# A graph kernel on one core: the node passes in sequence, x rows stored during the counting, messages weighed by column, and a small memset with a wait behind some gathers

## The chip, the cores and the metric

One NeuronCore of one Trainium2 chip. The metric is the device time of the whole kernel in microseconds (us), the median of several executions. The engines are PE (TensorE), DVE (VectorE), ACT (ScalarE), POOL (GpSimd) and SP (SyncE, which only issues DMAs here). POOL issues every gather and scatter by index, one indirect DMA for 128 rows.

## The reference, cut to what matters

N = 100,000 nodes with D = 64 features, E = 50,000 edges sorted by destination, 32 relations.

```python
edge_index = jnp.stack([src, dst])
h = jnp.maximum(_layernorm(x, axis=-1), 0.0)
x = x + _L0_gnn_ref(h, edge_index, W1, b1, W2, b2)       # two GCN layers
h = jnp.maximum(_layernorm(x, axis=-1), 0.0)
x = x + _L1_gnn_ref(h, edge_attr_64, src, dst, edge_type_32, rel_w, res_w1, res_w2)
# GCN layer: h = x @ W; agg[dst] += h[src] * dinv[src] * dinv[dst]; + h * dinv^2 + b
#   its edge_index are the inputs' src and dst; dinv = 1/sqrt(1 + count of dst)
# L1: att = sum(h_proj[etype, src] * tanh(h_proj[etype, dst] + efeat))
#     a = softmax of att over the edges of one destination
#     h_nb[dst] += h[src] * a
#     out = leaky((h + h_nb) @ res_w1.T) + leaky(h * h_nb @ res_w2.T)
```

## The kernel before

The edges lie in SBUF as 128 partitions by KE = 392 columns, and are handled in GE = 28 groups of GT = 14 columns. The nodes are handled in NB = 49 blocks of 2048 rows (128 partitions by CB = 16). Every engine has its own program, in the order in which it is written; they meet only at semaphores. `S["x"]`-like names are semaphores, `after(eng, sem, n)` is a wait that is left out for n <= 0. The stages, in order of time:

1. **Counting.** For each of the 392 edge columns DVE makes two fp16 one-hot rows (`lo_hot`, 128 wide, L454; `hi_hot`, 784 wide, L455) and PE multiplies them into PSUM, which gives the number of edges of each node. Four of each are in flight. Meanwhile POOL gathers the x rows of the destinations ("own" rows, L1201), 14 gathers to a group, into a ring of OWN = 5 buffers; SP stores each full group to `xd_t` (`keep_own`). In the SP program the first of these stores comes in the node stage, so POOL stops after five groups until then.
2. **Node stage.** Two passes over the 49 blocks. Pass t (`step_t`) normalises x and stores rows with the node's place (`node_rows`). Pass q (`step_q`) reads them back, multiplies by the weights on PE, adds x, normalises, and stores three arrays. `over_nodes` interleaves them on every engine: five t steps, then two t steps to one q step, then the remaining q steps. `own_after` says at which step SP does `keep_own(g)`.
3. **Edge stage e.** For each group POOL gathers the rows of the sources from `node_rows` into a ring of NBR = 6 buffers ("near" rows), and DVE sums them over equal destinations by a scan (`step_e`). POOL's near gathers come after its own gathers and after the last t rows are stored; the seventh group waits until DVE is through with the first (`S["d1"]`).
4. **Stage d** (second GCN layer) and **stage c** (neighbours gathered, 192-wide rows scattered to slots by relation), both with POOL busy from end to end.
5. **Scores.** PE, ACT and DVE compute the attention scores of the slots in two halves; POOL gathers the first half back (`score_got`, 196 gathers) while the second is computed, and then the second.
6. **Final stage f.** Softmax, then for each group on DVE (`step_f`): carry (L910), weighing of the rows by the softmax weight (L912), scan (L916), division by the sum (L922), sum and product with h (L926, L927), a masked sum (L929 to L931) for the edges that go on in the next partition, and `f_post` of the group before: leaky (L562), L900, L902. POOL then scatters 14 times to `out` (L1196). L902 waits for the scatter of two groups earlier, since `fout` has two buffers.

All DMAs of SP are issued in one line, the helper `load` (L977); the gathers are issued in L1201 and the scatters in L1196.

## Time and profile before

| | |
|---|---|
| median of 3 executions | 4637.77 us (4633.24 to 4641.26) |
| profiled execution, its own time | 4642.34 us |
| profiled execution, span | 4640.6 us |
| busy in it | POOL 3032.0 us (65%), DVE 2526.9 (54%), PE 1563.3 (34%), ACT 1012.3 (22%) |
| POOL on the chain that ended last | 48% of the span, and 16% more as "issue" |

The span runs from the first to the last instruction. "Issue" is time in which an engine waited for nothing that the profile shows; on POOL it is the gap of 0.30 us ahead of every indirect DMA. A busy share is an average over stages with different limits, so what counts is which engine is waited for in each stage.

### The profile page before, as it was taken

The page shows a single profiled execution, that of the slowest core. Times are in us where ns is not written, and L with a number is a line of the kernel's source. Part 1 is how long each engine was busy: PE and PEld are TensorE (multiplying, and loading weights), DVE is VectorE, ACT ScalarE, POOL GpSimd, SP SyncE. Part 2 cuts the span into 40 slices and gives each one's busy share as a digit, 9 for nine tenths or more (in the row PEclk, how much of TensorE's full clock was granted, in tenths as well). Part 3 has the DMA queues.
Part 4 walks back from the last instruction along what each step waited for, and adds up shares of the span by engine and source line. Part 5 has one row for each costly group of instructions (what it writes and reads, how often), then busy time and mean ns, then how long its engine had stood idle before and what let it go on. Part 6 is the DMA issues. An engine that isn't in the chain of part 4 may idle for free.

```text
span 4640.6 us, 31267 instructions
## 1 busy us (share of the span) xinstructions
PE 1563.3 (34%) x8094; PEld 1135.9 (24%) x8094; DVE 2526.9 (54%) x4033; ACT 1012.3 (22%) x1596; POOL 3032.0 (65%) x2761
## 2 busy tenths in 40 slices
PE   8835445688654340000000000023346600333331
PEld 2224334467543230000000000012335500322231
DVE  9967777777797666987741111112222200666663
ACT  0023333455432221111110000012222200222221
POOL 6026566640187776777757777777747777588887
PEclk9966666788776665555555555555556655666665
DMA  1056676776443334555532222234433300111110
GB/s 41 1 165 208 214 222 211 217 215 192 149 119 102 83 90 140 188 186 197 198 88 73 73 73 77 75 113 120 128 110 93 88 17 1 34 62 54 54 54 27
DMA packets 362638, 527.97 MB, mean 114 GB/s; under 512 B 220064, under 2 KB 232458, under 8 KB 362470
## 3 DMA queue, kind: packets, MB, share of 16 engines
q1 hardware_dynamic: 268166, 426.25, 28.2%
q0 software_dynamic: 94304, 99.74, 9.3%
q8 instruction: 74, 1.21, 0.1%
q14 instruction: 94, 0.77, 0.1%
HBM read 265.55 MB, written 264.24 MB: 114 GB/s over the span
## 4 chain that ended last, share of the span: by engine, by line
POOL 48%; issue 16%; PE 12%; DVE 11%; DMA 8%; ACT 2%; SPq 1%; POOLq 0%; DVEq 0%; ACTq 0%
POOL arena L1201 26%; POOL result L1196 10%; POOL slot_rows L1196 8%; DMA arena<-in_x 6%; POOL relf L1201 4%; PE banks L1534 3%; PE banks L1567 2%; PE banks L1669 2%; DMA work<-slot_rows 2%; PE banks L1559 1%; DVE arena L519 1%; SPq L977 1%; PE banks L1583 1%; DVE arena L455 1%; PE banks L1657 1%
## 5 line engine op out<-in xcount | busy, mean ns | idle before, releaser
L1201 POOL DMA_INDIRECT arena<-input_and_place_by_node,src_i x392 | 481.1, 1227 | 385.0 <-DVE arena L638 265.8
L1201 POOL DMA_INDIRECT work<-in_x,dsafe x392 | 414.1, 1056 | 435.6 <-DMA x_of_destination<-work 319.2
L1196 POOL DMA_INDIRECT result<-work,outi x392 | 502.1, 1281 | 164.3 <-issue 122.7
L1201 POOL DMA_INDIRECT arena<-g_by_node_and_edge,m_idx x392 | 445.1, 1136 | 121.1 <-issue 119.2
L1196 POOL DMA_INDIRECT slot_rows<-work,dsafe x392 | 404.3, 1031 | 141.7 <-issue 119.2
L1201 POOL DMA_INDIRECT arena<-h_by_node_and_edge,m_idx x392 | 405.3, 1034 | 119.5 <-issue 119.2
L1201 POOL DMA_INDIRECT relf<-slot_scores,src_i x392 | 369.9, 944 | 155.7 <-issue 128.5
L1657 PE MATMUL banks<-ident,work 128*128 128x128 f32 x456 | 111.5, 394 | 877.4 <-DMA work<-slot_rows 876.5
L819 DVE TENSOR_TENSOR work<-work,ends 128x896 f32<-128x896 f32 x28 | 46.7, 1668 | 568.1 <-DMA work<-h_by_node_and_edge 561.5
L1657 PEld LDWEIGHTS banks<-ident,work 128*128 128x128 f32 x456 | 80.3, 203 | 893.6 <-issue 696.0
L1669 PE MATMUL banks<-work 128*128 x912 | 209.6, 402 | 165.6 <-issue 115.1
L1567 PEld LDWEIGHTS banks<-w_sb,work 128*128 128x128 f32 x1568 | 224.4, 228 | 101.4 <-issue 101.4
L1567 PE MATMUL banks<-w_sb,work 128*128 128x64 f32 x1568 | 239.0, 316 | 0.0
L1669 PEld LDWEIGHTS banks<-work 128*128 128x128 f32 x912 | 180.0, 294 | 205.3 <-issue 205.3
L1699 PE MATMUL banks<-ident,work 128*128 128x128 f32 x392 | 90.5, 387 | 365.5 <-DVE work L927 365.5
L1553 PE MATMUL banks<-ident,arena 128*128 128x128 f32 x392 | 82.1, 347 | 388.3 <-DMA arena<-in_x 387.4
L1636 PE MATMUL banks<-last_run,carry 128*128 128x64 f32 (+1 forms) x6 | 1.8, 390 | 600.4 <-DVE last_run L775 593.2
L1534 PE MATMUL banks<-arena 128*128 128x392 f16 x784 | 195.6, 339 | 7.9 <-DVE arena L455 6.1
L833 DVE TENSOR_TENSOR dsti<-banks,work 128x256 f32<-128x256 f32 x57 | 24.2, 424 | 276.5 <-PE banks L1669 276.5
L1699 PEld LDWEIGHTS banks<-ident,work 128*128 128x128 f32 x392 | 72.2, 206 | 370.9 <-DVE work L927 370.9
L455 DVE TENSOR_SCALAR arena<-arena,pos 128x784 f16<-128x784 f16 x392 | 162.5, 415 | 0.0
L1553 PEld LDWEIGHTS banks<-ident,arena 128*128 128x128 f32 x392 | 59.7, 180 | 397.3 <-DMA arena<-in_x 341.6
(315 smaller groups left out, 5117.2 us busy)
## 6 DMA issues: line engine op xcount, KB each, us to landing
arena<-in_x SPq DMA_DIRECT2D x96, 512.0 KB, 5.3
slot_rows<-work SPq DMA_DIRECT2D x48, 912.0 KB
work<-slot_rows SPq DMA_DIRECT2D x114, 384.0 KB, 3.4
input_and_place_by_node<-arena SPq DMA_DIRECT2D x49, 528.0 KB, 2.9
arena<-input_and_place_by_node SPq DMA_DIRECT2D x49, 512.0 KB
g_by_node_and_edge<-arena SPq DMA_DIRECT2D x49, 512.0 KB, 3.3
h_by_node_and_edge<-arena SPq DMA_DIRECT2D x49, 512.0 KB, 3.1
arena<-x_of_destination SPq DMA_DIRECT2D x56, 448.0 KB, 4.3
```

The costliest lines, as they stand in the source:

```text
L455: ts(hi_hot[:, t % 4, :], iota_h, hi_key[:, t:t + 1], None, ALU.is_equal).then_inc(hot_made, 1)
L519: stt(out=trows[:, b % 2, :, 0:D], in0=cols(tx[:, b % 3]), scalar=0.0, in1=wide(st[:, 4, :], CB), op0=ALU.max, op1=ALU.mult).then_inc(T["h ...
L819: oc.did(tt(by_column(pd1)[:, 0:GT, :], cols(phd), wide(ends[:, group(g)], GT), ALU.mult))
L977: sp.dma_start(to, of).then_inc(signal, 16)
L1196: pool.indirect_dma_start(out=table[:, :], out_offset=bass.IndirectOffsetOnAxis(ap=idx, axis=0), in_=of, in_offset=None, bounds_check=boun ...
L1201: pool.indirect_dma_start(out=to, out_offset=None, in_=table[:, :], in_offset=bass.IndirectOffsetOnAxis(ap=idx, axis=0)).then_inc(signal, 16)
L1534: ins = matmul(bank(4 + k)[:, 0:KE], lo_hot[:, t % 4, :], hi_hot[:, t % 4, k * KE:(k + 1) * KE], start=t == 0, stop=t == KE - 1, skip_grou ...
L1553: ins = transpose(bank(0)[:, k * P:(k + 1) * P], qh0[:, b % 3, half + k * P:half + (k + 1) * P], ident[:])
L1567: ins = matmul(bank(4 + n % 2)[:, k * D:(k + 1) * D], qhid[:, n % 2, at:at + P], w2_sb[:], start=True, stop=True)
L1657: ins = transpose(bank(j % 2)[:, k * P:(k + 1) * P], slot_w[:, j % SB, k, D:RW], ident[:])
L1669: ins = matmul(bank(2 + j % 4)[:, at], slot_ht[:, q, at], flat[:, w], start=True, stop=True)
L1699: ins = transpose(bank(c % 2)[:, k * P:(k + 1) * P], ftwo[:, at:at + P], ident[:])
```

## The change

- `over_nodes` runs all t steps first, and then all q steps.
- SP stores the first OWN_EARLY = 12 own groups ahead of the node stage; the other 16 are stored at other steps than before.
- `lo_hot` is made once for 14 columns, by one `tensor_tensor` with both inputs broadcast, in a ring of two groups. Its keys are fp16.
- The near ring has NBR = 10 buffers; the four new ones lie over the own ring, so POOL waits ahead of group 6 until all own rows are stored.
- In stage f, ACT does the weighing, the division and the masking by one instruction for each of the 14 columns with a scale operand, and PE adds up the masked columns in PSUM. `f_post` of the group before moves between the scan and the sum and product.
- `gather_slowly` puts a memset of a [128, 2] tile and a wait for it behind the gather: in own groups 0 to 13, in near groups 0 to 9, and in the first half of the score gathers.
- Several semaphores are shared (`T` and `S` count on where `Q` and `G` had their own), with the same meaning.

```diff
             for b in range(NB + 1):
                 step_t(b)
-                if b >= 5 and b % 2:
-                    step_q((b - 5) // 2)
-            for k in range((NB - 5) // 2 + 1, NB + 4):
+            for k in range(NB + 4):
                 step_q(k)
...
-            for t in range(KE):
-                hot(t)
+            for g in range(GE):
+                after(dve, hot_used, (g - 1) * GT)
+                tt(lo_hot[g % 2], iota_h[:, 0:P].unsqueeze(1).to_broadcast([P, GT, P]), wide(lo_half[:, group(g)], GT, P),
+                   ALU.is_equal).then_inc(lo_made, 1)
+                for t in range(g * GT, (g + 1) * GT):
+                    after(dve, hot_used, t - 3)
+                    ts(hi_hot[:, t % 4, :], iota_h, hi_key[:, t:t + 1], None, ALU.is_equal).then_inc(hi_made, 1)
...
-                    of.did(tt(by_column(fd1)[:, 1:SC, 0:D], cols(arena[:, g * GW:(g + 1) * GW]), wide(weights, GT), ALU.mult))
                     of.did(v.tensor_copy(fd1[:, D * SC + 1:FW], weights))
                     of.wait()
                     dve.wait_ge(f["mat"], g + 1)
+                    dve.wait_ge(f["weighed"], g + 1)
+                    after(dve, f["masked"], g - 1)
...
-                    of.do(v.reciprocal(st[:, 1, :], st[:, 0, :]))
-                    of.do(tt(cols(fnb), by_column(run)[:, 1:SC, 0:D], wide(st[:, 1, :], GT), ALU.mult))
+                    v.reciprocal(st[:, 1, :], st[:, 0, :]).then_inc(f["share"], 1)
+                if g > 0:
+                    f_post(g - 1)
+                if g < GE:
+                    dve.wait_ge(f["nb"], g + 1)
...
-                    masked = fmask.rearrange("p (f t) -> p f t", t=GT)
-                    of.do(tt(masked, run.rearrange("p (f t) -> p f t", t=SC)[:, :, 1:SC], over_features(hm[:, group(g)], DW), ALU.mult))
-                    of.do(v.tensor_reduce(hs1[:], masked, AX.X, ALU.add))
-                    of.do(tt(hsum[:], hsum[:], hs1[:], ALU.add))
...
-                return [g for g in range(GE) if 8 + 7 * g // 4 == turn]
+                return [g for g in range(OWN_EARLY, GE) if 10 + 7 * (g - OWN_EARLY) // 2 == turn]
...
+            for g in range(OWN_EARLY):
+                keep_own(g)
             over_nodes(step_t, step_q)
...
+            rests = itertools.count(7)
+
+            def gather_slowly(to, table, idx, signal):
+
+                gather(to, table, idx, signal)
+                pool.memset(pause[:], 0.0).then_inc(consts, 1)
+                pool.wait_ge(consts, next(rests))
...
-                    gather(own[:, g % OWN, k * D:(k + 1) * D], x, dsafe[:, t:t + 1], own_got[g % OWN])
+                    (gather_slowly if g < GE // 2 else gather)(own[:, g % OWN, k * D:(k + 1) * D], x, dsafe[:, t:t + 1],
+                                                               own_got[g % OWN])
...
+                if g == 6:
+                    all_landed(pool, own_kept, OWN_KEPT)
                 after(pool, S["d1"], 2 * (g - NBR + 1))
...
-                    gather(near[:, g % NBR, k, :], node_rows, src_i[:, t:t + 1], near_got[g % NBR])
+                    (gather_slowly if g < NBR else gather)(near[g % NBR][:, k, :], node_rows, src_i[:, t:t + 1],
+                                                           near_got[g % NBR])
...
-                    gather(att[:, t:t + 1], att_t[k], score_row[:, t:t + 1], score_got)
+                    (gather if k else gather_slowly)(att[:, t:t + 1], att_t[k], score_row[:, t:t + 1], score_got)
...
+            def f_weigh(g):
+
+                after(act, f["run"], g)
+                for k in range(GT):
+                    t = g * GT + k
+                    ins = activation(by_column(fd1)[:, 1 + k, 0:D], arena[:, t * D:(t + 1) * D], ACT.Copy, scale=weight[:, t:t + 1])
+                ins.then_inc(f["weighed"], 1)
```

What SP issues at the end of its opening loads, before the change (`arena<-in_x` is a load of x for pass t, `input_and_place_by_node<-arena` a store of its rows, `arena<-input_and_place_by_node` a load for pass q):

```order
L977 DMA fix_two<-in_L_gnn_res_w 64x64 x2
L977 DMA arena<-in_x 128x1024
L977 DMA input_and_place_by_node<-arena 128x1056
L977 DMA arena<-in_x 128x1024
L977 DMA input_and_place_by_node<-arena 128x1056
```

The same place in the changed kernel (`x_of_destination<-work` is `keep_own`):

```order
L977 DMA fix_two<-in_L_gnn_res_w 64x64 x2
L977 DMA x_of_destination<-work 128x896 x12
L977 DMA arena<-in_x 128x1024
L977 DMA input_and_place_by_node<-arena 128x1056
L977 DMA arena<-in_x 128x1024
```

The twelve stores of own groups stand ahead of the load of the third x block; the loads of the first two stand ahead of them, among the opening loads.

DVE in one group of stage f, before the change:

```order
L910 COPY work<-work 128x65
L912 TENSOR_TENSOR work<-arena,tmp_a 128x14x64
L913 COPY work<-tmp_a 128x14
L916 SCALAR_TENSOR_TENSOR work<-work 128x975
L920 TENSOR_SCALAR estat<-work 128x14
L921 RECIPROCAL estat<-estat 128x14
L922 TENSOR_TENSOR work<-work,estat 128x896
L926 TENSOR_TENSOR work<-work 128x14x64
L927 TENSOR_TENSOR work<-work 128x14x64
L929 TENSOR_TENSOR work<-work,hm 128x910
L930 TENSOR_REDUCE hs<-work 128x65
L931 TENSOR_TENSOR hsum<-hsum,hs 128x65
```

And in the changed kernel (L565, L902 and L904 are `f_post` there, L919 the scan):

```order
L912 COPY work<-work 128x65
L914 COPY work<-tmp_a 128x14
L919 SCALAR_TENSOR_TENSOR work<-work 128x975
L923 TENSOR_SCALAR estat<-work 128x14
L924 RECIPROCAL estat<-estat 128x14
L565 SCALAR_TENSOR_TENSOR work<-work 128x1792
L902 TENSOR_TENSOR work<-work 128x896
L904 TENSOR_TENSOR work<-work 128x896
L932 TENSOR_TENSOR work<-work 128x14x64
L933 TENSOR_TENSOR work<-work 128x14x64
```

Weighing, division and masked sum are gone from DVE, and `f_post` stands ahead of the sum and product.

## Rows read from the trace of the kernel before

**Rows 1.** Busy time of each engine (with its instructions) in stretches of the span:

```profile
core 0: us, PE busy (x) PEld busy (x) DVE busy (x) ACT busy (x) POOL busy (x), PEclk, DMA share, GB/s
880.00:1230.00 350.00, 296.99 (x1860) 235.05 (x1859) 268.43 (x340) 191.78 (x309) 90.98 (x81) 0.86 0.66 203
1320.00:1420.00 100.00, 58.12 (x305) 41.06 (x306) 97.48 (x142) 35.90 (x57) 82.30 (x59) 0.74 0.40 121
1520.00:1620.00 100.00, 39.62 (x215) 28.51 (x215) 62.20 (x93) 25.24 (x40) 79.89 (x67) 0.67 0.33 88
3467.00:3717.00 250.00, 150.73 (x684) 123.39 (x684) 66.96 (x171) 53.94 (x114) 185.30 (x197) 0.63 0.33 91
4060.00:4600.00 540.00, 170.44 (x969) 155.31 (x969) 342.17 (x354) 110.06 (x206) 433.15 (x338) 0.66 0.17 53
```

**Rows 2.** Groups of POOL, 20 to 90 us: busy us, mean ns | idle before:

```profile
L1201 POOL DMA_INDIRECT work<-in_x,dsafe x56 | 54.6, 975 | 17.1 <-issue 17.1
```

**Rows 3.** Timeline of DVE, end of the counting: start us, us:

```profile
217.46 0.41 DVE L455 TENSOR_SCALAR arena<-arena,pos 128x784 f16<-128x784 f16 x1
217.80 0.24 DVE L454 TENSOR_SCALAR arena<-arena,m_idx 128x128 f16<-128x128 f16 x1
217.96 0.41 DVE L455 TENSOR_SCALAR arena<-arena,pos 128x784 f16<-128x784 f16 x1
```

**Rows 4.** Timeline of DVE, third block of pass t, and its fifth:

```profile
245.81 1.21 DVE L503 TENSOR_REDUCE t_stat<-arena 128x16 f32<-128x1024 f32 x1
...
265.08 1.23 DVE L519 SCALAR_TENSOR_TENSOR arena<-arena,t_stat 128x1024 f32<-128x1024 f32 x1
```

**Rows 5.** Line L519, the row product of pass t, over the span:

```profile
L519 DVE SCALAR_TENSOR_TENSOR arena<-arena,t_stat x49: 1225/1226/1227, 243.3 to 869.1; 128x1024 f32<-128x1024 f32 x49
```

**Rows 6.** Timeline of DVE, L544 of pass q in blocks 0, 22 and 48:

```profile
292.48 1.23 DVE L544 TENSOR_TENSOR arena<-arena,q_stat 128x1024 f32<-128x1024 f32 x1
...
880.37 1.22 DVE L544 TENSOR_TENSOR arena<-arena,q_stat 128x1024 f32<-128x1024 f32 x1
...
1230.09 1.23 DVE L544 TENSOR_TENSOR arena<-arena,q_stat 128x1024 f32<-128x1024 f32 x1
```

**Rows 7.** Timeline of stage e: its first instructions, two groups, the last gather:

```profile
1250.66 0.11 DVE L591 MEMSET arena<- 128x64 f32 x1 [3.71 <-DMA result<-work]
...
1261.34 2.35 POOL L1201 DMA_INDIRECT arena<-input_and_place_by_node,src_i  x1 [265.83 <-DVE arena L638]
...
1326.28 1.69 DVE L638 TENSOR_TENSOR arena<-arena 128x896 f32<-128x896 f32 x1
...
1339.85 1.68 DVE L638 TENSOR_TENSOR arena<-arena 128x896 f32<-128x896 f32 x1
...
1740.11 0.94 POOL L1201 DMA_INDIRECT arena<-input_and_place_by_node,src_i  x1 [0.30 <-issue]
```

**Rows 8.** Timeline of POOL, last gather of the first score half, first of the second:

```profile
3714.77 0.96 POOL L1201 DMA_INDIRECT relf<-slot_scores,src_i  x1 [0.30 <-issue]
3716.68 0.94 POOL L1201 DMA_INDIRECT relf<-slot_scores,src_i  x1 [0.96 <-DMA slot_scores<-tmp_b]
```

**Rows 9.** Timeline of the start: a memset on POOL, and its first gather:

```profile
0.31 0.10 POOL L1735 MEMSET const-float32-0.0<- 128x1 f32 x1 [0.31 <-issue]
...
5.03 0.36 DVE L399 TENSOR_SCALAR dsafe<-key 128x392 int32<-128x392 f32 x1
...
5.68 1.17 POOL L1201 DMA_INDIRECT work<-in_x,dsafe  x1 [2.23 <-DVE dsafe L399]
```

**Rows 10.** Timeline of stage f, one group:

```profile
4239.06 1.09 DVE L902 TENSOR_TENSOR work<-work 128x896 f32<-128x896 f32 x1 [7.43 <-DMA result<-work,outi]
...
4241.31 1.29 POOL L1196 DMA_INDIRECT result<-work,outi  x1 [0.30 <-issue]
...
4245.20 1.91 POOL L1196 DMA_INDIRECT result<-work,outi  x1 [0.30 <-issue]
...
4250.88 0.98 POOL L1196 DMA_INDIRECT result<-work,outi  x1 [0.30 <-issue]
```

More of the change, by code:

```diff
@@ L174, in build @@
         h_last = sb("h_last", [P, D])
+        pause = sb("pause", [P, 2])
         arena = sb("arena", [P, KE * D])
@@ L196, in build @@
         trows = part(arena, 4 * BW, [2, CB, TW])
-        near = part(arena, 0, [NBR, GT, TW])
+        near = [part(arena, k * GT * TW, [GT, TW]) for k in range(6)]
         sum2 = part(arena, 0, [SUM2, GT, D])
@@ L201, in build @@
         iota_h = part(arena, Q0, [KN], F16)
-        lo_hot = part(arena, Q0 + KN // 2, [4, P], F16)
-        hi_hot = part(arena, Q0 + KN // 2 + 2 * P, [4, KN], F16)
-        H0 = Q0 + KN // 2 + 2 * P + 2 * KN
+        lo_hot = [part(arena, Q0 + KN // 2 + k * GT * P // 2, [GT, P], F16) for k in range(2)]
+        hi_hot = part(arena, Q0 + KN // 2 + GT * P, [4, KN], F16)
+        lo_half = part(arena, Q0 + KN // 2 + GT * P + 2 * KN, [KE], F16)
+        H0 = Q0 + KN // 2 + GT * P + 2 * KN + KE // 2
         iota_i = part(arena, H0, [KN], I32)
@@ L240, in build @@
         own = part(work, 0, [OWN, GW])
+        near += [part(work, k * GT * TW, [GT, TW]) for k in range(NBR - 6)]
         W0 = OWN * GW
@@ L266, in build @@
         frun = part(work, 2 * FW, [2, FW])
-        fmask = part(work, 4 * FW, [DW * GT])
+        fmask = part(work, 4 * FW, [GT, DW])
         F0 = 4 * FW + DW * GT
@@ L327, in build @@
         sum2_got = ring("sum2_here", SUM2)
-        G = sems("d", "steps d1 mat run x1 centered square var std h")
+        G = sems("d", "steps d1 mat run x1 h")
         d_in, d_x1, d_h = ring("d_loaded"), ring("d_x1_stored"), ring("d_h_stored")
@@ L338, in build @@
         soft = sem("softmax_steps")
-        f = sems("f", "steps mat run two turned t o os half out")
+        f = sems("f", "steps mat weighed run share nb two masked summed turned t o os half out")
         f_in, f_sent = ring("f_loaded"), ring("f_sent")
@@ L1023, in step_t @@
                     load_x(b + 2)
+                for g in own_after(b):
+                    keep_own(g)
             def load_q(b):
@@ L1406, in _ @@
                 act.wait_ge(near_got[g % NBR], 16 * GT * (g // NBR + 1))
-                copy(m_idx[:, group(g)], near[:, g % NBR, :, D]).then_inc(S["place"], 1)
+                copy(m_idx[:, group(g)], near[g % NBR][:, :, D]).then_inc(S["place"], 1)
                 if g + 1 < GE:
@@ L1716, in _ @@
                     f_residual(g, c)
-            carried(7, DW, 2)
+                pe.wait_ge(f["masked"], g + 1)
+                for k in range(GT):
+                    ins = matmul(bank(7)[:, 0:DW], ident[:], fmask[:, k, :], start=g == 0 and k == 0, stop=False,
+                                 skip_group_check=True)
+                ins.then_inc(f["summed"], 1)
+            pe.wait_ge(fix["ve"], at_step["last run 2"])
+            matmul(bank(7)[:, 0:DW], carry[:], last_run[:], start=False, stop=True,
+                   skip_group_check=True).then_inc(fix["pe"], 1)
             pe.wait_ge(fix["ve"], at_step["fix operands"])
```

93 lines of the change are left out of this document (53 added, 40 removed).

## The prediction, as it was put on record

> **What bounds the kernel now.** I read first the windows, for who is busy in each stage, and then the timelines, for what a stage's steps cost. In the later pass q (880 to 1230) PE, DVE and the DMAs are all well filled [rows 1]. In stage e DVE is busy 97 of 100 us at first, with 59 gathers; 200 us later DVE has 62 and POOL 67 gathers in 100 us, one per 1.49 us: the bound has passed from DVE to POOL [rows 1]. In the score gathers POOL runs without a pause, and the last gather of the first half ends only 1.0 us (3716.68 less 3714.77 + 0.96) before the second half may start, on whose DMA it waits 0.96 us [rows 8]. So that half has no slack. In stage f POOL has 338 instructions in 540 us, 22.4 us per group of 14, with DVE at 63% [rows 1]: POOL is the bound there.
>
> **The rest behind a gather.** It is a memset and a wait for it. A memset takes 0.10 us [rows 9]. The gap of 0.30 us ahead of each gather stands there with no wait, and the first gather starts 0.29 us after DVE's end at 5.39 that released it [rows 9]; so a wait may be free within the gap, or cost one more. The rest is thus 0.10 to 0.40 us. That POOL's own signal is quicker than another engine's is not shown; I take the middle, **r = 0.25**. Should a signal take POOL as long as the 0.96 us it waited at the half's end, r would be nearer 0.6; I keep that for the tail.
>
> **Counting and early stores.** A column costs DVE 0.34 + 0.16 = 0.50 us [rows 3]; 28 batches for `lo_hot` take at most 1.226 x 1792/1024 = 2.1 us each [rows 5] in place of 14 x 0.16 = 2.2. That ends the counting some 3 to 6 us sooner, near 212 rather than 218; batches at double rate would end it some 30 us sooner. It hardly matters: SP now stores own group 11 before it loads the third x block, and that needs 168 gathers. The pitch of own gathers is 0.975 + 0.305 = 1.28 us [rows 2]; with r it is 1.53. Each batch is a two-input DVE operation of 2 us. What such a one may do to POOL is seen in stage f, where one scatter of a group takes 1.91 and another 0.98 [rows 10]. About 1.2 us lost in each 7 us of counting is 0.26 per gather: 1.79. From 22 (218 less 196) to 212 that makes 106, with 11 before; the other 51 at 1.53 take 78 us, so the 168th ends near 291 to 295, and with a few us for its store and the load, the third block is at L503 at about 300, not at 245.81 [rows 4]: **54 us late**. Without rests it would be near 250, hardly late; with r = 0.4, near 325.
>
> **Node passes alone.** Pass t alone steps at (265.08 - 243.3)/4 = 5.44 us [rows 4, 5], pass q alone at (1230.09 - 880.37)/26 = 13.45 [rows 6]. From the fifth t row product to the first L544 are 27.4 us, and from the last L544 to stage e's start 20.6 [rows 6, 7]. Today the 44 other t steps and 22 q steps take 869.1 - 265.08 = 604 us [rows 4, 5]; alone they would take 44 x 5.44 + 22 x 13.45 = 535. So the sequence is 50 to 69 us shorter, the late third block eats it: 300 + 3 + 47 x 5.44 + 27 + 48 x 13.5 + 21 = **1257** for stage e's start against 1250.66, that is +7 (the 3 us are from L503 to the row product, an estimate). In general it is the end of the 168th gather less 288. The cost of t and q alone is taken from few or late blocks; that q runs as fast from block 0 as from block 22 rests on PE's clock, 0.86 granted there [rows 1].
>
> **Near ring.** Near gathers start today at 1261.34, after a wait for L638 [rows 7], with six groups ready; in the change ten are. Group 6 waits for all own rows stored, about q step 12, long before 1257, so these waits and the rests of 140 near gathers (35 us) lie under pass q and cost nothing; left uncovered they would cost these 35. DVE takes 1339.85 - 1326.28 = 13.57 us a group [rows 7], and POOL 14 x 1.69 = 23.7 while DVE is busy, 14 x 1.49 = 20.9 later [rows 1]. DVE catches up with POOL after k groups where 13.57 (9 + k) = 11 + 23.7 k, k = 11; the remaining 7 of POOL's 18 groups go at 20.9. Stage e's gathers then end 11 + 260 + 147 = 418 us after its start. The last one ends 1741.05 - 1250.66 = 490 us after it now [rows 7], and the same sum for six ready groups and 22 to gather gives 486 (k = 5.6). So **-71**: four groups less are worth less than 4 x 20.9 = 84, because more of the rest fall beside a busy DVE. The bounds are -84, and -52 if the dear pitch lasts to the end (18 x 23.7).
>
> **Scores.** The 196 gathers of the first half each take r more, and the half had 1.0 us to spare [rows 8]: 196 x 0.25 - 1 = **+48** (+19 at 0.10, +77 at 0.40). What the rest gives back, for example to DMAs of the stage beside it, would have to come from the second half, which is ready without it.
>
> **Stage f.** Six scatters of a group's 14 overlap two-input DVE work today. The group's scatters cost 1.29, 1.91 and 0.98 in [rows 10], so L912 and the weight division L922, now on ACT, hold at most (1.29 - 0.98) + (1.91 - 0.98) = 1.24 us per group, 35 in all. `f_post` moves too, and may hold others instead; I take 0.8, **-22** (0 to -50). ACT gets 42 instructions per group and is busy 110 of 540 us now [rows 1], so 17.8 of 22.4 us are free: up to 0.42 us each they fit. DVE loses six operations and stays under POOL. If ACT's cost 0.5, ACT and not POOL would pace the stage, at about 25 us a group, +70.
>
> **Sum.** +7 - 71 + 48 - 22 = -38. The profiled execution took 4642.3, 4.6 above the median of 4637.8, so against its own time the result is 4604, against the median 4600; I give **4600**. Per 0.1 of r the time moves by about 35 us (168 own gathers, of which the node stage feels all, and 196 score gathers): r = 0.10 gives 4547, 0.40 gives 4650, and the change breaks even at r near 0.36.
>
> **A rule against it.** The own gathers beside the one-hots, each a one-input fp16 operation of 0.41 us, take 975 ns [rows 2, 3], against 0.94 where DVE leaves POOL alone [rows 8]; a gather is thus hardly held there, and the sum holds with that. The memset between them is another kind of POOL instruction, and may be held for the rest of such an operation, 0.2 us on average: 115 of them would cost 23 us more, 4623. The Trainium skill (SBUF — State Buffer, "Who interferes with whom") has that rule: a one-input DVE operation in a two-port mode locks the port pair it shares with GpSimd for the whole instruction. The row on the gathers does not agree with it; on the memset no run here speaks yet.
>
> **Rivals.**
> (a) The rest is nearly free, r at most 0.12: the gap before each gather already holds it. For it speaks that the 0.30 gap has no wait to explain it, so that a wait may lie inside it. At 0.10 the node term is 7 - 0.15 x 168 = -18 and the score term +19, the sum -92: 4546, or 4530 to 4560 over stage f's bounds.
> (b) The rest costs 0.4 to 0.6: a wait for a signal comes on top of the gap, as it does at 3716.68, 0.96 after POOL was free, of which an unknown part is the DMA's [rows 8]. The place is the first score half and the 168 own gathers; from r = 0.36 the change loses. At r = 0.5: 7 + 0.25 x 168 = +49, -71, +97, -22, about 4690.
> (c) Pass q alone from block 0 finds PE at the lower clock. PE is busy 297 of 350 us at 0.86 granted [rows 1]; near 0.6 its share of a block would go from 11.4 to over 16.5. With 48 blocks at 3.1 more: +149, about 4750. Against it: 26 blocks alone ran at 0.86.
> (d) The memset held by one-hots, above: 4623; or ACT too slow in stage f, near 4670.
>
> **Chances.** Forecast 0.45, with its own range 4570 to 4635 (r 0.2 to 0.3 and the bounds of stages e and f); (a) 0.20; (b) 0.20, of which half lies above 4675; (c) 0.04; (d) 0.11. The range, 4535 to 4675, leaves out the best of (a), half of (b), and (c): about 0.2. A measurement of this kernel tells about 0.2%, 9 us, from no change. Faster: most of the forecast and of (a), part of (d), 0.64; same, 4628 to 4647: 0.12; slower: (b), (c), the rest of (d), 0.24.
>
> **What would show it.** The start-to-start pitch of own gathers (1.53 in place of 1.28 while no batch runs) and of the first score half (196 gathers ending 48 us late, the second half waiting for none of its DMAs) gives r. The third t block at L503 near 300; the row products of pass t 5.44 apart; L544 13.5 apart from the first; stage e's gathers ending 418 us after its start; 21.6 us per group in stage f, with ACT below it. The prediction is wrong if the rest is outside 0.2 to 0.3, if q alone is not 13.5, or if DVE in stage f no longer leaves time, because two scatters' worth of `f_post` comes ahead of the sum.

## The result, and the profile after

The changed kernel takes 4491.19 us (median of 4, 4477.68 to 4499.61) against 4635.51 of the kernel before in the same set (a set is measured together on one chip, and the kernel before is always in it): ratio 0.9686, 95% interval [0.9658, 0.9714], 144 us less. The prediction had 4600 and a range of 4535 to 4675: the sign was right, the size far off, and the time lies 44 us below the range. The profiled execution has a span of 4492.4 us, 148 less than that of before.

The stages read from the two timelines, in us of the span:

| | before | after | forecast for after |
|---|---|---|---|
| third block of pass t at its first reduce (L503, now L506) | 245.81 | 285.44 | 300 |
| last row product of pass t | 869.1 | 541.5 | 558.7 |
| one block of pass q alone | 13.45 (26 blocks) | 12.36 (48 blocks) | 13.5 |
| start of stage e | 1250.66 | 1181.15 | 1257 |
| from there to the end of the last near gather | 490.4 | 419.9 | 418 |
| stage c, its first gather to its last scatter | 1070.5 | 1062.2 | 1070.5 |
| first score half, first gather to the second half's first | 249.4 | 266.8 | 297 |
| from the last score gather to the first scatter of stage f | 41.0 | 45.9 | 41 |
| the 392 scatters of stage f | 625.4 | 602.6 | 603 |

First POOL, in the counting and after it. The timeline of the changed kernel shows a gather (L1202), the memset of its rest (L1210) and the next gather, with the time POOL was idle before it:

```profile
62.74 0.95 POOL L1202 DMA_INDIRECT work<-in_x,dsafe  x1 [0.27 <-POOL pause L1210]
63.69 0.11 POOL L1210 MEMSET pause<- 128x2 f32 x1
64.07 2.15 POOL L1202 DMA_INDIRECT work<-in_x,dsafe  x1 [0.27 <-POOL pause L1210]
66.22 0.22 POOL L1210 MEMSET pause<- 128x2 f32 x1
66.71 0.95 POOL L1202 DMA_INDIRECT work<-in_x,dsafe  x1 [0.27 <-POOL pause L1210]
...
275.25 0.95 POOL L1202 DMA_INDIRECT work<-in_x,dsafe  x1 [0.27 <-POOL pause L1210]
276.20 0.11 POOL L1210 MEMSET pause<- 128x2 f32 x1
276.58 0.95 POOL L1202 DMA_INDIRECT work<-in_x,dsafe  x1 [0.27 <-POOL pause L1210]
```

The idle time ahead of a gather is 0.27 us behind the wait, where it was 0.30 without one [rows 2]: the wait lies inside the gap, and a rest costs its memset less 0.03. With DVE idle the gathers start 1.33 us apart, so r is 0.08. A gather that meets a batch of `lo_hot` takes 2.15 in place of 0.95, the 1.2 us forecast; a memset that meets one keeps its 0.11.

A memset that meets a one-hot of `hi_hot` (L461) takes 0.22:

```profile
25.00 0.47 DVE L461 TENSOR_SCALAR arena<-arena,pos 128x784 f16<-128x784 f16 x1 [0.23 <-PE banks L1578]
25.29 0.22 POOL L1210 MEMSET pause<- 128x2 f32 x1
```

It ends at 25.51, 0.03 us after the one-hot, and so do all 83 such memsets in which a one-hot was under way: they start 0.23 to 0.30 us into it and last until it is over. DVE pays too. 14 one-hots take 5.01 us here and 4.75 in the kernel without rests (no_rests, below):

```profile
65.32 5.01 DVE L461 TENSOR_SCALAR arena<-arena,pos 128x784 f16<-128x784 f16 x14
```

```profile
63.84 4.75 DVE L461 TENSOR_SCALAR arena<-arena,pos 128x784 f16<-128x784 f16 x14
```

The last one-hot ends at 214.3 with the rests and at 207.3 without them, against 218.4 before. The change hides these 7 us behind the next wait.

The timeline of DVE shows what the early stores cost:

```profile
231.27 1.22 DVE L506 TENSOR_REDUCE t_stat<-arena 128x16 f32<-128x1024 f32 x1
...
285.44 1.22 DVE L506 TENSOR_REDUCE t_stat<-arena 128x16 f32<-128x1024 f32 x1 [43.47 <-DMA arena<-in_x]
```

DVE stands 43.5 us for the third x block. SP issues its load only when the 168th own gather is over, at 277.5.

Then the two passes, one line of the program each over the span (count, shortest, median and longest in ns, first and last start):

```profile
L522 DVE SCALAR_TENSOR_TENSOR arena<-arena,t_stat x49: 1225/1226/1227, 239.4 to 541.5; 128x1024 f32<-128x1024 f32 x49
L547 DVE TENSOR_TENSOR arena<-arena,q_stat x49: 1224/1224/1226, 566.8 to 1160.0; 128x1024 f32<-128x1024 f32 x49
```

and pass q in the windows, in the form of [rows 1], once from its first block to its last:

```profile
core 0: us, PE busy (x) PEld busy (x) DVE busy (x) ACT busy (x) POOL busy (x), PEclk, DMA share, GB/s
566.83:1159.99 593.16, 510.38 (x3393) 403.25 (x3392) 491.70 (x621) 352.06 (x567) 185.70 (x293) 0.91 0.69 218
```

48 blocks in 593.2 us are 12.36 each, with a granted clock of 0.91, where the 26 blocks of before had 13.45 and 0.86 [rows 1]. What a block costs at either clock is seen in PE's timeline. L1611 are the 16 products of a half block:

```profile
955.40 1.06 PE L1627 MATMUL banks<-res_sb,work 128*128 128x128 f32 x8
959.52 1.12 PE L1597 MATMUL banks<-ident,arena 128*128 128x128 f32 x4 [3.06 <-DMA arena<-in_x]
...
962.57 3.67 PE L1611 MATMUL banks<-w_sb,work 128*128 128x64 f32 x16
966.04 1.06 PE L1619 MATMUL banks<-ident,arena 128*128 128x128 f32 x4
966.89 1.91 PE L1627 MATMUL banks<-res_sb,work 128*128 128x128 f32 x8
968.60 0.71 PE L1597 MATMUL banks<-ident,arena 128*128 128x128 f32 x4
...
970.29 2.00 PE L1611 MATMUL banks<-w_sb,work 128*128 128x64 f32 x16
...
973.47 0.60 PE L1597 MATMUL banks<-ident,arena 128*128 128x128 f32 x4
```

PE stood 3.06 us for a load of x, and then the 16 products took 3.67 us, at 1.2 GHz (a window of 960 to 962 shows a granted clock of 0.50; it fell during the pause), in place of 2.00 at 2.4. From its first transposes (L1597) to those of the next, this half block took 9.08 us, and the next one 4.87. DVE stood behind it:

```profile
962.72 1.22 DVE L547 TENSOR_TENSOR arena<-arena,q_stat 128x1024 f32<-128x1024 f32 x1
969.46 1.23 DVE L565 SCALAR_TENSOR_TENSOR work<-work 128x1024 f32<-128x1024 f32 x1 [5.51 <-ACT work L1353]
```

ACT's copy L1353 waits for PE's L1627. So by the difference of the two half blocks 4.2 of DVE's 5.51 us are the lower clock; the rest goes with the late load. A block at full clock takes 11.25 us and is paced by DVE, which is busy 10.25 of them; the block that began at 962.7 took 16.86. Pass q is a mixture: most blocks take 11.2 to 12.3, the 11 dear ones 13.6 to 17.1, and the mean goes by how often a dear one comes (the first two take 8.9). In this trace the 16 products of a half block ran at the lower clock 9 times in 48 blocks, each time behind a pause of PE of 1.7 to 3.3 us. The granted clock itself fell 19 times in these windows; some falls met other products. In the trace of before such products came 9 times in the last 26 blocks, where the pauses went up to 5.1 us.

Last, the scores and stage f:

```profile
3319.35 0.99 POOL L1202 DMA_INDIRECT relf<-slot_scores,src_i  x1 [26.82 <-DMA slot_scores<-pos]
...
3586.16 0.95 POOL L1202 DMA_INDIRECT relf<-slot_scores,src_i  x1 [0.27 <-POOL pause L1210]
3587.41 0.94 POOL L1202 DMA_INDIRECT relf<-slot_scores,src_i  x1 [0.30 <-issue]
```

The gather at 3586.16 is the first of the second half; the last rest stands ahead of it. The first half runs 1.36 us apart where it ran 1.27 apart, and the second half follows without the wait for its DMA that stood in [rows 8]: 17.4 us more, all on the path.

```profile
3882.00:4485.00 603.00, 360.80 (x1898) 342.10 (x1897) 242.50 (x276) 434.37 (x1348) 479.33 (x393) 0.65 0.19 54
```

In this window of stage f ACT is busy 434 of 603 us, 15.5 of 21.5 per group, and POOL has 393 instructions: POOL still sets the period. ACT's timeline gives the 14 single-column instructions of each kind:

```profile
3851.24 3.50 ACT L1527 ACTIVATE work<-arena,tmp_a 128x64 f32<-128x64 f32 x14
3857.57 4.18 ACT L1534 ACTIVATE work<-work,estat 128x64 f32<-128x64 f32 x14 [2.84 <-DVE estat L924]
...
3872.34 4.21 ACT L1543 ACTIVATE work<-work,hm 128x65 f32<-128x65 f32 x14
```

They are 0.25 to 0.30 us each. The first weighing stands on the path, since the first scan of stage f waits for it, and so does the first division:

```profile
3854.86 2.19 DVE L919 TENSOR_TENSOR_SCAN work<-work 128x975 f32<-128x975 f32 x1 [4.23 <-ACT work L1527]
...
3861.79 1.09 DVE L932 TENSOR_TENSOR work<-work 128x896 f32<-128x896 f32 x1 [4.25 <-ACT work L1534]
```

The scan starts 18.7 us after the last score gather, and 16.0 after it in before. That is 2.7 of the 4.9 us more ahead of the first scatter; the rest comes in ACT's steps behind it.

### The profile page after: what moved, and what is told of

Its sections match the earlier page's. It is cut to its first block, busy times and chain, and to the rows that moved or that the text cites. A ratio compares the mean times of both kernels' runs of the same rounds, so it can differ in the third digit from the quotient of the medians.

```text
span 4492.4 us, 34467 instructions
## 1 busy us (share of the span) xinstructions
PE 1605.1 (36%) x8878; PEld 1252.6 (28%) x8878; DVE 2361.7 (53%) x3528; ACT 1340.0 (30%) x2772; POOL 3099.8 (69%) x3293
## 4 chain that ended last, share of the span: by engine, by line
POOL 53%; issue 18%; DVE 16%; PE 5%; DMA 4%; ACT 3%; SPq 1%; POOLq 0%; DVEq 0%; ACTq 0%
POOL arena L1202 21%; POOL result L1197 9%; POOL slot_rows L1197 8%; POOL relf L1202 8%; POOL work L1202 6%; DMA arena<-in_x 3%; DVE arena L522 1%; DVE arena L508 1%; POOL pause L1210 1%; DVE t_stat L513 1%; DVE t_stat L506 1%; PE banks L1611 1%; DVE arena L538 1%; DVE work L565 1%; DVE arena L561 1%
## 5 line engine op out<-in xcount | busy, mean ns | idle before, releaser
L1202 POOL DMA_INDIRECT arena<-input_and_place_by_node,src_i x252 | 313.2, 1243 | 461.0 <-DVE arena L641 386.5
L1197 POOL DMA_INDIRECT result<-work,outi x392 | 479.3, 1223 | 169.2 <-issue 122.1
L1202 POOL DMA_INDIRECT arena<-g_by_node_and_edge,m_idx x392 | 447.0, 1140 | 121.1 <-issue 119.2
L1202 POOL DMA_INDIRECT work<-in_x,dsafe x392 | 432.9, 1104 | 117.1 <-issue 62.3
L1202 POOL DMA_INDIRECT arena<-h_by_node_and_edge,m_idx x392 | 400.7, 1022 | 119.5 <-issue 119.2
L1202 POOL DMA_INDIRECT relf<-slot_scores,src_i x392 | 371.2, 947 | 150.1 <-issue 68.3
L1701 PE MATMUL banks<-ident,work 128*128 128x128 f32 x456 | 112.1, 395 | 874.3 <-DMA work<-slot_rows 873.2
L1701 PEld LDWEIGHTS banks<-ident,work 128*128 128x128 f32 x456 | 81.1, 204 | 890.2 <-issue 689.6
L565 DVE SCALAR_TENSOR_TENSOR work<-work 128x1024 f32<-128x1024 f32 (+1 forms) x77 | 116.6, 1514 | 298.3 <-ACT work L1520 238.9
L1611 PEld LDWEIGHTS banks<-w_sb,work 128*128 128x128 f32 x1568 | 197.6, 205 | 82.0 <-issue 82.0
L1763 PE MATMUL banks<-work,ident 128*128 128x65 f32 x784 | 170.9, 413 | 118.6 <-ACT work L1543 118.6
L1611 PE MATMUL banks<-w_sb,work 128*128 128x64 f32 x1568 | 211.3, 292 | 0.0
L1202 POOL DMA_INDIRECT work<-input_and_place_by_node,src_i x140 | 173.5, 1239 | 50.8 <-issue 34.1
L1597 PE MATMUL banks<-ident,arena 128*128 128x128 f32 x392 | 68.0, 301 | 392.6 <-DMA arena<-in_x 391.6
L1763 PEld LDWEIGHTS banks<-work,ident 128*128 128x128 f32 x784 | 165.7, 325 | 123.9 <-ACT work L1543 123.9
L1441 ACT COPY arena<-arena 128x896 f32<-128x896 f32 x28 | 47.8, 1708 | 408.5 <-DMA arena<-g_by_node_and_edge,m_idx 408.5
```

The source lines that it names most:

```text
L565: return stt(out=to, in0=of, scalar=0.01, in1=of, op0=ALU.mult, op1=ALU.max)
L1197: pool.indirect_dma_start(out=table[:, :], out_offset=bass.IndirectOffsetOnAxis(ap=idx, axis=0), in_=of, in_offset=None, bounds_check=boun ...
L1202: pool.indirect_dma_start(out=to, out_offset=None, in_=table[:, :], in_offset=bass.IndirectOffsetOnAxis(ap=idx, axis=0)).then_inc(signal, 16)
L1441: copy(by_column(ed1[:, g % 2])[:, 1:SC, :], sum2[:, g % SUM2]).then_inc(G["d1"], 1)
L1597: ins = transpose(bank(0)[:, k * P:(k + 1) * P], qh0[:, b % 3, half + k * P:half + (k + 1) * P], ident[:])
L1611: ins = matmul(bank(4 + n % 2)[:, k * D:(k + 1) * D], qhid[:, n % 2, at:at + P], w2_sb[:], start=True, stop=True)
```

## The experiments

Sixteen more runs were made, in four sets: ten other kernels, the change once more, and five of the ten a second time. A ratio is to the kernel before in the same set. "Traced" is from each run's own profile.

### One part undone or done alone

**No rests at all.** The changed kernel without

```diff
-                pool.memset(pause[:], 0.0).then_inc(consts, 1)
-                pool.wait_ge(consts, next(rests))
```

> The changed kernel with no memset and no wait behind any gather; nothing else is altered. Theory 1, the rests only cost: the first score half takes 249.5 us again in place of 268.1 (-18.6), the first twelve own groups are gathered some 15 to 25 us sooner and pass t starts that much earlier, so about 4455 to 4460 us in all against 4491. Rival, the rests are what makes pass q faster than forecast (12.36 us per block against the 13.45 of before) because POOL's traffic lies differently beside it: then a block of pass q costs about 13.45 again, +52 us, and the sum is about +15: 4505 us.

Measured: 0.9612 [0.9595, 0.9629], 4463.8 us. Traced: first half 248.4 us, 168th own gather over at 263.2, 12.33 us a block in pass q with a clock of 0.90 in the last 26. Theory 1 holds; the rests don't speed pass q. The half took 18.4 us less than in the change, whose half is 266.8 and not the 268.1 of the expectation.

**Rests in the first score half, on the kernel before.** The tile is declared ahead of `arena`, as in the change.

```diff
+        pause = sb("pause", [P, 2])
...
                     gather(att[:, t:t + 1], att_t[k], score_row[:, t:t + 1], score_got)
+                    if k == 0:
+                        pool.memset(pause[:], 0.0).then_inc(consts, 1)
+                        pool.wait_ge(consts, 7 + t - HALF)
```

> The kernel before, with a memset and a wait behind each of the 196 gathers of the first score half and nowhere else. Theory 1: the start-to-start pitch there goes from 1.25 to 1.34 us, so +18 us on 4635.5, about 4653. Rival, the rest gives something back to the second half or to the transfers beside it: no change within 9 us. Up to its scores the program is that of before, so its trace is also a second look at pass q alone: if a block costs 13.4 us there again, the slow pace belongs to the kernel before; if it costs 12 to 12.8, it is chance of one execution.

Measured: 1.0003 [0.9990, 1.0017], but traced the half is 267.4 us, 18 longer. Pass q alone took 12.93 us a block. The time is that of the rival, and the trace that of theory 1; the sets further down explain this.

**The order of the node passes, with its early stores, on the kernel before.** Nothing else is altered.

```diff
-                if b >= 5 and b % 2:
-                    step_q((b - 5) // 2)
-            for k in range((NB - 5) // 2 + 1, NB + 4):
+            for k in range(NB + 4):
...
-                return [g for g in range(GE) if 8 + 7 * g // 4 == turn]
+                return [g for g in range(12, GE) if 10 + 7 * (g - 12) // 2 == turn]
...
+            for g in range(12):
+                keep_own(g)
```

> The kernel before with the node passes in sequence and own groups stored as in the change (twelve ahead of the node stage); no rests, no batched one-hots, six near buffers, stage f of before. Theory 1, pass q alone really costs some 12.4 us a block in this order: third t block near 250, stage e starts near 1145 in place of 1250.7, about -105 us: 4530. Rival, 12.4 needs the rests or the batched one-hots and a block is 13.45 here: stage e starts near 1195, about -55 us: 4580. Second rival, the late own groups hold up SP in pass q: over 4590.

Measured: 0.9826 [0.9807, 0.9845], 4568.6 us, 77 less. Traced: third block at 249.9, pass q 12.82 us a block (clock 0.88), stage e at 1169.7, 81 us earlier. It lies between the theories: a block costs less than 13.45 without rests or batches, but more than 12.4.

**Six near buffers in the changed kernel.**

```diff
-NBR = 10
+NBR = 6
```

> The changed kernel with six near buffers in place of ten; all else is the change. Theory 1, ten ready groups are worth what stage e got shorter by: from stage e's start to the last near gather 490 us again in place of 420, so +70: 4561. Rival, stage e got shorter for another reason and the ring only adds memory: less than +20.

Measured: 0.9812 [0.9795, 0.9829]. Traced: stage e's gathers end 498.4 us after its start, against 419.9 with ten. The ring is worth 78 us between these two traces, and 0.0126 of 4640, 58 us, beside the ratio of the change, with 15 us of uncertainty either way. Over all traces outside the next set, this stretch takes 490 to 498 us in the six kernels and runs with six buffers and 420 to 427 in the eight with ten, 72 us less on the mean. Theory 1 holds.

**The next four** fell on a chip on which the kernel before takes 5225.0 us. There PE stands for stretches in which it waits for nothing the trace shows. This is the list of waits of tile_alone in the counting (23 to 278 us), total, times and longest:

```profile
PEld banks L1535 <- issue: 67.0, 30, 5.5
PE banks L1535 <- issue: 55.5, 13, 4.8
DVE arena L455 <- remote: 55.2, 12, 5.0
```

The counting took 60 us more than in [rows 3] by that, and the second score half was ready 235 us after POOL. Stages e and f were as long as elsewhere (496.6 and 625.1 us in tile_alone), but stage c took 1223 to 1227 us in place of 1060 to 1071, though POOL is busy in it from end to end elsewhere. So of this set only stage f is used for the other chips, and its three other kernels were run again.

**The tile alone, on the kernel before.**

```diff
         h_last = sb("h_last", [P, D])
+        pause = sb("pause", [P, 2])
```

> The kernel before with the 8-byte tile pause declared ahead of arena and work, and never used; no instruction is added. It asks why 196 rests in the score half, 18 us longer there in the trace, left the time of score_rests at 1.0003 of before. Theory L, the tile shifts arena and work in SBUF and stage c (1070 us in before, 1060 to 1063 in every kernel with the tile) and pass q get shorter: 0.996 to 0.998 of before, 8 to 17 us less. Rival, the stages differ from execution to execution and the layout does nothing: 1.000 within 0.0015.

Measured: 1.0005 [0.9981, 1.0029]; too wide for 10 us.

**No rests in the scores, and no rests behind own gathers,** each in the changed kernel:

```diff
-                    (gather if k else gather_slowly)(att[:, t:t + 1], att_t[k], score_row[:, t:t + 1], score_got)
+                    gather(att[:, t:t + 1], att_t[k], score_row[:, t:t + 1], score_got)
```

> The changed kernel without the rests in the first score half; own and near rests stay. Theory 1, each costs its 0.09 us since POOL alone paces that half: 18 us less than the change, ratio to before about 0.9648. Rival, by score_rests a rest there costs nothing in time: 0.9686, as the change.

Measured: 0.9592 [0.9551, 0.9632]. The half took 479 us, 232 of them a wait for the second half's scores, so rests would have been hidden there. The changed kernel itself was not in this set, so the ratio has nothing to stand beside.

```diff
-                    (gather_slowly if g < GE // 2 else gather)(own[:, g % OWN, k * D:(k + 1) * D], x, dsafe[:, t:t + 1],
-                                                               own_got[g % OWN])
+                    gather(own[:, g % OWN, k * D:(k + 1) * D], x, dsafe[:, t:t + 1], own_got[g % OWN])
```

> The changed kernel without the rests behind own gathers; near and score rests stay. Theory 1: the 168th own gather ends at 263 in place of 277.5, the node stage starts 14 us sooner and nothing takes it back: ratio about 0.9656. Rival, the third x block waits for something else: 0.9686.

Measured: 0.9503 [0.9460, 0.9547], again without the changed kernel beside it. Traced, the 168th own gather is over at 263.6 and the third block at 270.0, against 277.9 and 285.8 in no_score_rests on the same chip: theory 1 in the trace.

**Stage f alone, on the kernel before.** All edits of stage f from the change (DVE, ACT and PE); its core is

```diff
-                    of.did(tt(by_column(fd1)[:, 1:SC, 0:D], cols(arena[:, g * GW:(g + 1) * GW]), wide(weights, GT), ALU.mult))
...
+                    dve.wait_ge(f["weighed"], g + 1)
...
+            def f_weigh(g):
...
+                f_normal(g)
...
+                        f_masked(g)
```

> The kernel before with stage f alone changed (weighing, division and masking on ACT by column, masked sum on PE, f_post ahead of the sum and product). Theory 1: the scatters of stage f take 602 us in place of 625, and the first one comes 5 us later, since ACT weighs the first group ahead of the first scan: -18 us, ratio 0.996. Rival, part of the 23 us belongs to the other edits: over 0.998.

Measured: 0.9954 [0.9929, 0.9979], 24 us less. Traced: 599.7 us for the scatters against 625.1 of tile_alone on the same chip. Ahead of them stand 45.5 us, but tile_alone has 45.9 there, so the 5 us later start of theory 1 is not seen on this chip; on the others it is 41 us in the five traces without the change of stage f and 45.8 to 46.9 in the nine with it. The time and the scatters are as theory 1 has them.

### The rests again, and PE's pauses

> The changed kernel itself once more, as the yardstick of this set and as another look at pass q. Theory: ratio 0.9686 within 0.004; in pass q the blocks take 11.25 us where PE runs at 2.4 GHz and 15 to 17 where it is granted half of it for part of the block, and the number of such blocks differs from the last execution.

Measured: 0.9671 [0.9656, 0.9687], 4485.1 us, as at first. Traced: 11.88 us a block, in the windows

```profile
567.32:1137.80 570.48, 488.80 (x3394) 384.80 (x3393) 491.28 (x620) 351.47 (x567) 191.79 (x293) 0.95 0.70 227
```

The same program had 593.2 us for the same 48 blocks at a clock of 0.91, and has 570.5 at 0.95: 23 us between two executions, and the two spans differ by 24.4.

> The changed kernel without the rests in the first score half, again, since in the last set PE and not POOL paced that half. Theory 1: 18 us less than after_again, ratio to before about 0.9648. Rival, by score_rests these rests cost nothing: equal to after_again within 0.002.

Measured: 0.9625 [0.9610, 0.9641], 0.0046 or 21 us under after_again; traced 248.1 us for the half in place of 266.7. Theory 1 holds.

> The changed kernel without the rests behind own gathers, again. Theory 1: the 168th own gather ends 14 us sooner and pass t starts that much sooner: 14 us less than after_again, ratio about 0.9656. Rival: equal to after_again within 0.002.

Measured: 0.9613 [0.9598, 0.9628], 27 us under after_again. Traced: 168th own gather over at 262.8, third block at 269.3 in place of 285.7: 16 us. The rest of the 27 is within the two intervals. Theory 1 holds.

**Transposes twice.**

```diff
-                for k in range(4):
+                for k in (0, 1, 2, 3, 0, 1, 2, 3):
                     ins = transpose(bank(0)[:, k * P:(k + 1) * P], qh0[:, b % 3, half + k * P:half + (k + 1) * P], ident[:])
```

> The changed kernel with the four transposes ahead of the hidden layer of pass q done twice into the same bank, which adds 0.6 us of PE work at 2.4 GHz to each half block and shortens PE's waits there; the result is the same. In the change PE's clock fell at 960 us behind a wait of 3.06 us for the x rows. Theory C, such waits are what lets the clock fall: fewer slow blocks, pass q under 12.0 us a block, 15 to 30 us less than after_again. Rival, PE's work is what counts, as a slow block is one that PE paces: the 1.2 us a block (2.2 at half clock) come on top of the slow ones, pass q over 12.6, 10 to 50 us more than after_again.

Measured: 0.9670 [0.9657, 0.9683], the same as after_again. Traced, windows of its 48 blocks:

```profile
570.82:1156.94 586.12, 528.95 (x3769) 426.66 (x3769) 492.01 (x621) 353.78 (x567) 181.91 (x291) 0.94 0.69 221
```

Both theories missed: 12.21 us a block lies between them, and between the two traces of the unaltered kernel. PE has some 19 to 40 us more work than in those two, and the pass is no longer for it: at full clock DVE covers it. PE's pauses over 2 us were 10, against 16 and 16 in the unaltered kernel; the granted clock fell 9 times, against 19 and 10. So the pauses were made rarer, and the falls came out as rare as in the better of the two executions and rarer than in the other: one trace can't tell whether the edit did that.

### Layout or chance

> The kernel before with the unused 8-byte tile ahead of arena and work, again: its first run fell on a chip on which PE stood for long stretches and every kernel took 10% more, so it could not tell 10 us. Stage c, from its first gather to the last slot scatter, was 1070.5 and 1066.7 us in the two traces without the tile and 1060 to 1064 in the eight with it. Theory L, the layout is worth it: stage c under 1064 us again and 0.996 to 0.9985 of before in time. Rival, chance of two traces: ratio 1.000 within 0.0015.

Measured: 0.9967 [0.9955, 0.9980], 4624.1 us: an unused tile of 8 bytes per partition makes the kernel before 15 us faster. Traced: stage c 1062.1 us, pass q 12.54 a block in the last 26. Theory L holds in time and in stage c.

> The kernel before with the rests in the first score half, again. Theory L: 18 us more than tile_alone_2, since both have the tile. Rival, the rests cost nothing in this kernel: equal to tile_alone_2 within 0.0015. If it is 18 us more than before and tile_alone_2 equals before, the first run of it was off by chance.

Measured: 0.9992 [0.9983, 1.0002], 0.0025 over tile_alone_2, 12 us, with 7 us of uncertainty either way; traced 267.3 us for the half. So the first run of it was not off by chance: the rests cost it 12 to 18 us and the tile that they need gave 15 back.

> The changed kernel without any rest, again, as the yardstick for nine_early, and to see it beside the runs with one set of rests taken away (0.9625 without those of the scores, 0.9613 without the own ones). If the two add up: 0.957. If it stays at 0.961, they do not, and what is read as the worth of one set is in part chance of pass q.

Measured: 0.9589 [0.9575, 0.9604], 38 us under after_again. That lies halfway between the two values of the expectation. The two sets of rests, 21 and 27 us by their runs and 18.6 and 16 in the traces, add up to 48 and 35, and the four ratios leave some 14 us of uncertainty: they may add up. The near rests were never taken away alone; in the trace of the change the last of them ends at 805, long before stage e.

**Nine groups stored ahead of the node stage,** in the kernel of no_rests:

```diff
-OWN_EARLY = 12
+OWN_EARLY = 9
```

> The changed kernel without rests, and OWN_EARLY = 9 in place of 12. In no_rests the third x block still came 34.8 us after DVE was ready for it, since SP first waits for 168 own gathers. Theory 1, that wait is all on the path: with 126 gathers, ended by about 205, the third block is at 236 to 240 and all later stages 32 us earlier, 4430 us or 0.954. Rival, own groups stored later get in the way of pass t or q, or keep POOL from the near gathers: no better than no_rests_2.

Measured: 0.9549 [0.9533, 0.9565], 4432.7 us, the fastest of all and 0.0040, 19 us, under no_rests_2. DVE no longer waits for the third block, which is at 235.57 against 269.7 in no_rests_2:

```profile
230.13 1.21 DVE L506 TENSOR_REDUCE t_stat<-arena 128x16 f32<-128x1024 f32 x1
235.57 1.21 DVE L506 TENSOR_REDUCE t_stat<-arena 128x16 f32<-128x1024 f32 x1
241.00 1.21 DVE L506 TENSOR_REDUCE t_stat<-arena 128x16 f32<-128x1024 f32 x1
```

Pass t ends 34 us earlier (491.6 against 525.8), stage e starts 18.5 earlier (1142.4 against 1161.0): pass q took 604.6 us in place of 587.9. So theory 1 holds for the third block and pass t, and half of its gain is lost in pass q, in its first 22 blocks: 13.25 us each at a clock of 0.84, against 12.42 at 0.92, and after them 12.04 against 12.10. Those are the blocks beside which own groups are stored in this kernel (to the 24th, against the 13th), as the rival had it; but two executions of one program differ as much, so the stores are not shown as the cause.

## Why the prediction was right or wrong

By its own steps, in us against the span of before:

**Rest, r = 0.25.** Wrong in size: 0.08 with DVE idle, 0.09 in the scores, and 0.19 where the memset takes 0.22. The prediction named the row that decides, the gap of 0.30 that stands without a wait, and then took the middle of its two readings. The wait fits inside the gap, so r is the memset less 0.03; rival (a) had the mechanism. The scores paid 17.4 in place of 48. Of the first 168 rests 84 took 0.22 and the others mostly 0.11, which is 84 x 0.06 + 84 x 0.17 = 19 us less than at 0.25. Gathers held by DVE's two-input work lost 35 us in place of the 30 allowed. The 14 us that are left fit the 14.6 by which the third block came sooner than 300. The held memset of rival (d) is there, at about half its price: 0.11 where it allowed 0.2 on average, since the rests always came late in a one-hot. What no one forecast is that DVE is held as well, 7 us over the counting. The Trainium skill (SBUF — State Buffer, "Who interferes with whom") has it that a DVE instruction in a two-port mode takes the shared ports for its whole length and fully blocks the other engine. If the one-hots run in such a mode, the memsets agree, each ending 0.03 us after the one-hot it met; the gathers beside the same one-hots, at 0.95, do not.

**Early stores.** Right in mechanism: SP held the third x block for the 168th gather, 40 us late in place of 54, by r. The counting ended at 214.3, near the 212 forecast, but for two errors that cancel: without rests it ends at 207.3, 11 us sooner and not 3 to 6, and the rests take 7 back. no_rests_2 and nine_early show that this wait was on the path: 34 us in pass t.

**Pass t alone, 5.44 a block.** Right, 5.39.

**Pass q alone, 13.45 to 13.5 a block.** This is the step that failed most: 12.36 measured, 48 blocks, 55 us. The prediction took the mean of 26 blocks of one execution as the price of a block. It was no price but a mixture. With r at its measured size the prediction's own sum gives about 4554, inside its range; pass q takes the time out of it.

The last 26 blocks in all fourteen traces outside the slow chip, in us a block:

| | old order | new order |
|---|---|---|
| without the tile `pause` | 13.45 (before) | 12.64 (order_alone) |
| with it | 12.93, 13.05, 12.54; mean 12.84 | 11.52 to 12.42 in nine traces; mean 12.01 |

So some 0.8 us a block go with the order, in both rows, and the runs don't say by what; that POOL's near gathers lay beside the first of the 26 in the old order is one difference. Some 0.6 us go with the tile or with the execution: each kernel without the tile has one trace, and two traces of the changed kernel, 12.11 and 11.52, differ as much. The time goes with the clock granted in those blocks, with up to 0.4 us of scatter: 13.45 at 0.86, 13.05 at 0.88, 12.42 at 0.90, 12.10 at 0.93, 11.81 at 0.95 and 11.52 at 0.98. Rival (c) had the mechanism with the wrong sign: it asked what a lower clock than 0.86 would cost, and not what a higher one would give. The blocks in [rows 1] were there to be listed one by one: 15 of them take 11.2 to 12.1, and 11 take 14.1 to 18.3.

**Near ring, -71.** Right: 70.5 between the two traces, 78 by near_six's trace, 72 on the mean of all; and the near rests lay under pass q, as forecast.

**Stage f, -22.** Right: 22.7 in the trace, and 25 alone. What it left out is the 4.9 us ahead of the first scatter, where ACT's steps of the first groups stand on the path.

**Stage c and layout.** Not in the prediction. The tile `pause` shifts `arena` and `work`; alone it is worth 15 us [9, 21]. Of it 8 us are seen in stage c: 1070.5 and 1066.7 us in the two traces without the tile, 1060.3 to 1064.7 in the twelve with it outside the slow chip. The 392 gathers there take 6.4 us less in tile_alone_2 than in before, though as many, 36, take over 1.1 us. First tile_alone_2, then before:

```profile
L1202 POOL DMA_INDIRECT arena<-h_by_node_and_edge,m_idx x392 | 398.9, 1017 | 119.5 <-issue 119.5
```

```profile
L1201 POOL DMA_INDIRECT arena<-h_by_node_and_edge,m_idx x392 | 405.3, 1034 | 119.5 <-issue 119.2 <-ACT work L1455 0.3
```

Why the layout does that, and where the other 7 us go, stays open; pass q, above, may hold them.

**The sum.** Forecast -38, in the trace -148.2. The differences: pass q -55, start of pass t -15, the shorter fill and pass t -4, scores -31, stage c -8, first groups of stage f +5, and -2 because the terms of stage e's start add up to 1254.7 and not to 1257: -110 of the 110. What stays open is what makes the clock fall. In the stretches of pass q alone of the fourteen traces, 56 of 61 pauses of PE over 3 us came with a fall of the granted clock, during the pause or within 2.6 us of its end, and so did 74 of 144 pauses of 2 to 3 us and 24 of 100 of 1.3 to 2 us. So longer pauses go with falls more often, but a pause alone does not decide. The rests, which the change puts in three stretches, cost about 35 us of what it could have gained; no run shows a gain by them.

## What to carry to other kernels

Before the mean of a stretch is used as the price of a step, list its steps: where two prices alternate (here 11.25 and 14 to 18 us, the dear ones with part of the block at 1.2 GHz in place of 2.4), the mean is a matter of how often the dear one comes, and goes with the execution. When a store is moved ahead of a load in a queue, count what the store waits for: without rests, twelve early groups held the passes for 34 us, and nine held them not at all, though half of that was lost again in pass q. And when an edit adds a tile, run the tile alone: 8 bytes gave back about what the 196 rests cost that they came with.

## What the runs showed of the hardware that was not expected

- A wait of POOL for its own memset is covered by the gap that each indirect DMA has anyway: 0.27 us idle behind the wait, 0.30 without one.
- POOL's memset takes 0.11 us, and 0.22 us where it meets one of DVE's fp16 one-hots of 784 elements: 83 memsets all ended 0.03 us after the one-hot under way. In that kernel 134 of the 392 one-hots took 0.44 to 0.49 us in place of 0.41, against one in the kernel without rests. A gather beside them takes 0.95 us and is not held; beside a two-input batch of 2.01 us it takes 2.15, and there the memset keeps its 0.11.
- An unused tile of 8 bytes per partition ahead of the large buffers: 0.9967 [0.9955, 0.9980] of the time.
- PE stood for 3.06 us, and then a half block took 9.08 us at 1.2 GHz in place of 4.87 at 2.4. Over fourteen traces the mean block of pass q went from 11.5 to 13.45 us as the granted clock went from 0.98 to 0.86.
- One chip ran the four kernels that also ran elsewhere 11 to 13% longer (the kernel before 5225.0 in place of 4641 us). PE stood up to 5.5 us at a time in the counting for nothing that the trace shows, and its granted clock there (23 to 278 us) was 0.85, where it is 1.00 in the trace of before (23 to 218 us).
